# The projection of the next batch is computed beside the recurrence's chunks, and GpSimd issues the token loads

## The chip, the cores and the metric

The program runs on one core of one Trainium2 chip. A core has TensorE (PE in the rows), VectorE (DVE), ScalarE (ACT), GpSimd (POOL) and SyncE (SP), which here only issues transfers. Each takes its own instructions in order, and they wait for one another by semaphores. The metric is the device time of one execution in microseconds (us); lower is better.

## What is computed

A convolutional recurrence over an image turns `x` into `x1`, sixteen images of 64 channels and 1024 positions. Then comes a state-space layer over the 1024 positions ("tokens") of each image, and a layer of experts. The change touches the state-space layer. Cut down, with `x` the normalised tokens of a batch of 16:

```python
x_proj = x @ W_in                     # 64 -> 2*128
xs, z = jnp.split(x_proj, 2, axis=-1)
delta, Bv, Cv = xs @ W_delta, xs @ W_B, xs @ W_C
deltaA = jnp.exp(jnp.einsum('bld,dn->bldn', delta, A))
deltaB = jnp.einsum('bld,bln->bldn', delta, Bv)
def step(state, inp):                 # over the 1024 tokens
    dA_i, dB_i, x_i, C_i = inp
    state = dA_i * state + dB_i * x_i[:, None, :]
    return state, jnp.einsum('bdn,bn->bd', state, C_i)
y = (ys of the scan) * jax.nn.silu(z)
return y @ W_out
```

A state has 128 x 128 numbers in each batch.

## The kernel before

Five parts run one behind the other, parted by barriers: the convolution (`conv_phase`), the projection (`build_project`), the recurrence (`build_scan`), the gate (`build_gate`) and the experts. They pass data through tensors in HBM.

**The projection** goes over the 16 batches as a software pipeline (`pipelined`): the pieces of batches n to n-3 stand beside each other, all eight PSUM banks are in use, and two buffers of everything alternate. A batch is loaded (`px`), its mean over channels is taken and removed, squared, the variance is made by a second product, and ACT (square root) and DVE (reciprocal, product) normalise it. `xs` and `z` are made for the two halves of 512 positions, and from `xs` the rates (`delta`), the readout (`Cv`), and, with the roles of weights and data exchanged so that tokens lie on partitions, the steps (`delta` again), `own` (`xs` itself) and `Bv`; own times `Bv` is what enters. Rates, steps and entering tokens are each split into three bf16 parts (a cast, the rest, its cast, the rest of that), which are stored to `rates_dram`, `steps_dram` and `tokens_dram`; later products of parts restore near-f32 accuracy.

**The recurrence** cuts the tokens of a batch into 17 chunks: `CROWD` = 16 of 63 tokens and a last one of 16 (`CPB` = 17). A chunk has `GROUPS` = 8 units of 16 channels. For each unit `g` of chunk `c`

- PE makes in `enters` what enters the state into `enter_ps` (8 matmuls on loaded `steps` and `tokens`; two buffers, so it waits until the scan before the last one is done), and in `exponents` the exponents of the unit after it into `rate_ps` (4 matmuls); in the even units it contracts the states of the chunk before with the readout (`contract`: 4 matmuls on 32 columns each, into `y_ps`),
- ACT copies the end state of the chunk before into column 0 of `enter_ps` (`carry`) and takes two exponentials of the next unit (`decays_of`, into `decay`, a ring of four),
- DVE runs one `tensor_tensor_scan` over 128 x 1024 elements.

POOL spreads the loaded rates of a chunk over four masked copies (`s_wide`) and the readout into a sparse operand (`spread`). It does both once in a chunk, in the order widen, spread. SP issues the loads of a chunk three chunks ahead (`load`): 1 for rates, 8 for tokens (L797), 16 for steps (L801), 1 for the readout, and every second chunk 4 stores of y. Before the tokens it waits until PE has used up the buffers of the chunk two before. y is summed in two PSUM banks `y_ps[0]` and `y_ps[1]`, of two chunks each, and ACT moves each sheet out (`move_y`). The batch loop is a hardware loop (`Fori`) of 136 unrolled units.

Of the kernel before, what the change touches and what calls it, by code (L numbers as in the profile page):

```python
# [5 lines left out]
F32 = mybir.dt.float32  # L6
# [6 lines left out]
BATCH = 16  # L13
CH = 64
# [347 lines left out]
def gate_phase(nc, y_dram, z_dram, x1_dram, w_out, mean_w, identity, gate_w, gate_b, x2_dram, normed_dram, logit_dram):  # L362
    def scratch(name, shape, dt=F32):
# [8 lines left out]
    build_project(nc, identity=identity, readout_dram=readout, rates_dram=rates, steps_dram=steps, tokens_dram=tokens,  # L372
                  **held["project"])
    build_scan(nc, identity=identity, readout_dram=readout, rates_dram=rates, steps_dram=steps, tokens_dram=tokens,
               decays_dram=decays, y_dram=y, **held["scan"])
    build_gate(nc, y, z_dram, x1_dram, w_out, mean_w, identity, gate_w, gate_b, x2_dram, normed_dram, logit_dram)


def build_project(nc, x1_dram, w_in, w_delta, w_b, w_c, mean_w, readout_dram, z_dram, identity,
                  rates_dram, steps_dram, tokens_dram):  # L380

    with ExitStack() as ctx:
        def sb(name, shape, dt=F32):
            return ctx.enter_context(nc.sbuf_tensor(name, shape, dt))

        sem = Semaphores(nc, ctx, "proj")
        win = sb("win", [128, CHUNKS, 2 * INNER])
        wdelta, wc, wmean = sb("wdelta", [INNER, INNER]), sb("wc", [INNER, INNER]), sb("wmean", [128, 128])  # L390
        wtok = sb("wtok", [INNER, 3, 128])
        eps = sb("eps", [128, 1])
        x = [sb(f"px{i}", [128, BANK]) for i in range(2)]
        centred, square, std = sb("centred", [128, BANK]), sb("square", [128, BANK]), sb("std", [128, BANK])
        normed = [sb(f"normed{i}", [128, BANK]) for i in range(2)]
        xs = [sb(f"xs{i}", [INNER, CHUNKS, BANK]) for i in range(2)]
        z = [sb(f"z{i}", [INNER, CHUNKS, BANK]) for i in range(2)]
        readout = [sb(f"readout{i}", [INNER, CHUNKS, BANK]) for i in range(2)]
        parts = [sb(f"parts{i}", [INNER, SPLITS, CHUNKS, BANK], BF16) for i in range(2)]
        rest = [sb(f"rest{c}", [INNER, BANK]) for c in range(CHUNKS)]  # L400
        own = [sb(f"own{c}", [128, TILES, INNER]) for c in range(CHUNKS)]
        enters = [sb(f"enters{c}", [128, TILES, STATE]) for c in range(CHUNKS)]
        enters_left = [sb(f"enters_left{c}", [128, TILES, STATE]) for c in range(CHUNKS)]
        steps_left = [sb(f"steps_left{c}", [128, TILES, INNER]) for c in range(CHUNKS)]
        steps = [sb(f"steps{i}", [128, CHUNKS * TILES, SPLITS, INNER], BF16) for i in range(2)]
        tokens = [sb(f"tokens{i}", [128, CHUNKS * TILES, SPLITS, STATE], BF16) for i in range(2)]

        def ps(name):
            return ctx.enter_context(nc.psum_tensor(name, [128, BANK], F32))

        mean_ps, var_ps, xs_ps, zc_ps, delta_ps = (ps(n) for n in ("mean_ps", "var_ps", "xs_ps", "zc_ps", "delta_ps"))
        tok_ps = [ctx.enter_context(nc.psum_tensor(n, [128, TILES, 128], F32)) for n in ("step_ps", "own_ps", "b_ps")]

        weights_in, eps_set = sem("weights_in"), sem("eps_set")
        x_in = [sem(f"x_in{i}") for i in range(2)]
        stored = [sem(f"stored{i}") for i in range(2)]
        tok_stored = [sem(f"tok_stored{i}") for i in range(2)]
        mean_ready, centred_ready, square_ready, var_ready, std_ready = (
            sem("mean"), sem("centred"), sem("square"), sem("var"), sem("std"))
        inverse_ready, normed_ready = sem("inverse"), sem("normed")  # L420
        in_ready, xs_ready, z_ready = sem("in_ready"), sem("xs_ready"), sem("z_ready")
        out_ready, part1_ready, rest1_ready, part2_ready, part3_ready = (
            sem("out_ready"), sem("part1"), sem("rest1"), sem("part2"), sem("part3"))
        readout_ready = sem("readout")
        own_ready = sem("own")
        tok_ready, enters_ready, step1_ready, token1_ready, step_left, token_left, step2_ready, token2_ready, tok3_ready = (
            sem("tok"), sem("enters"), sem("step1"), sem("token1"), sem("step_left"), sem("token_left"), sem("step2"),
            sem("token2"), sem("tok3"))
        STORES = 2 + SPLITS
        TOK_STORES = 1 + SPLITS  # L430
        WEIGHTS = 6 + CHUNKS
        block = ctx.enter_context(nc.Block())

        def of_chunk(tile, c, a):
            return tile[:, TILES * c:TILES * c + TILES, a, :]

        @block.sync
        def _(sp):
            for s in sem.made:
                sp.sem_inc(s, START)  # L440
            for d, s in ((wdelta, w_delta), (wc, w_c), (wmean, mean_w)):
                sp.dma_start(d[:, :], s).then_inc(weights_in, DMA)
            for k, s in enumerate((w_delta, identity, w_b)):
                sp.dma_start(wtok[:, k, :], s).then_inc(weights_in, DMA)
            for c in range(CHUNKS):
                sp.dma_start(win[:, c, :], w_in[c, :, :]).then_inc(weights_in, DMA)

            def load(b, i, turn):
                sp.wait_ge(centred_ready, START + turn * 2)
                for c in range(CHUNKS):  # L450
                    sp.dma_start(x[i][CH * c:CH * c + CH, :],
                                 x1_dram[bass.ds(b, 1), :, BANK * c:BANK * c + BANK].rearrange("b c l -> (b c) l")
                                 ).then_inc(x_in[i], DMA)

            def store(b, i, turn):
                sp.wait_ge(z_ready, START + (b + 1) * CHUNKS)
                sp.dma_start(z_dram[bass.ds(b * CHUNKS, CHUNKS), :, :].rearrange("n p l -> p n l"), z[i][:, :, :]
                             ).then_inc(stored[i], DMA)
                sp.wait_ge(readout_ready, START + (b + 1) * CHUNKS)
                sp.dma_start(readout_dram[bass.ds(b, 1), :, :].rearrange("b n l -> (b n) l"),  # L460
                             readout[i][:, :, :].rearrange("p c l -> p (c l)")).then_inc(stored[i], DMA)
                sp.wait_ge(part3_ready, START + (b + 1) * CHUNKS)
                for a in range(SPLITS):
                    dst = rates_dram[bass.ds(b, 1), :, SPLITS * a:SPLITS * a + terms_of(a), :]
                    sp.dma_start(dst.rearrange("b d e l -> (b d) e l"),
                                 parts[i][:, 0:terms_of(a), :, :].rearrange("p a c l -> p a (c l)")
                                 ).then_inc(stored[i], DMA)
# [208 lines left out]
def build_scan(nc, readout_dram, a_t, identity, rates_dram, steps_dram, tokens_dram, decays_dram, y_dram):  # L676
# [4 lines left out]
    with ExitStack() as ctx:  # L681
# [85 lines left out]
        def _(sp):  # L767
            for s in sem.made:
                sp.sem_inc(s, SCAN0)
# [824 lines left out]
```

## Time and profile before

| | us |
|---|---|
| median of 3 runs | 7372.27 (7366.63 to 7378.81) |
| the profiled execution | 7362.99 |
| its span in the trace | 7361.1 |
| convolution, to the last vector instruction | 0 to 1885.6 |
| projection and the set-up of the recurrence, to the first scan | 1885.6 to 2277.1 |
| recurrence, first to last large scan | 2277.1 to 7007.2 |
| gate, experts | 7030 to 7361 |

Busy time over the span: PE 6408.9 (87%), DVE 6478.1 (88%), ACT 4524.9 (61%), POOL 2747.4 (37%). These shares are means over parts with different limits; what bounds a part is read within it. The execution is one core's, with a mean granted TensorE clock of 0.97 of full speed.

### The profile page before, as it was taken

To read this page: it belongs to the slowest core of one execution; us is meant where nothing else is said; L and a number is where in the kernel's file an instruction comes from. 1 tells how busy PE (TensorE), PEld (TensorE's weight loads), DVE (VectorE), ACT (ScalarE), POOL (GpSimd) and SP (SyncE) were. 2 spreads that over 40 slices of the span, in tenths; PEclk is the share of its full clock that TensorE was granted. 3 is DMA by queue.
4 is the path that set the end of the run, shared out by engine and by line. 5 is a ranking of instruction groups with operands and counts; after the bars stand their busy time and mean duration, and the time that the engine had idled before them with its cause. 6 is when DMAs were issued, how large, how long until landed. Compare 5 with 4: busy or idle time off the path is not lost. (4 is left out here: it accounts for less than half of the span.)

```text
span 7361.1 us, 173597 instructions
## 1 busy us (share of the span) xinstructions
PE 6408.9 (87%) x52385; PEld 3911.8 (53%) x52385; DVE 6478.1 (88%) x4166; ACT 4524.9 (61%) x9561; POOL 2747.4 (37%) x1996
## 2 busy tenths in 40 slices
PE   8999999999786888888888888888888888888867
PEld 3555547555344555555555555555555555555535
DVE  7888878888557999999999999999999999999962
ACT  7888868888464555555555555555555555555541
POOL 5555445555234333333333333333333333333300
PEclk9999999999898999999999999999999999999985
DMA  6666666666693111111111111111111111111154
GB/s 144 153 156 154 155 144 155 154 154 155 199 321 83 27 27 27 28 27 27 28 26 27 28 27 28 27 27 28 27 26 28 26 29 27 27 27 28 27 171 113
DMA packets 918664, 569.20 MB, mean 77 GB/s; under 512 B 710606, under 2 KB 819054, under 8 KB 917870
## 3 DMA queue, kind: packets, MB, share of 16 engines
q1 hardware_dynamic: 917885, 560.17, 32.1%
q8 instruction: 325, 5.32, 0.3%
q14 instruction: 454, 3.71, 0.2%
HBM read 161.99 MB, written 125.17 MB: 39 GB/s over the span
## 5 line engine op out<-in xcount | busy, mean ns | idle before, releaser
L1059 DVE TENSOR_TENSOR_SCAN states<-decay,enter_ps 128x1024 f32<-128x1024 f32 x2048 | 4468.2, 2262 | 172.3 <-ACT enter_ps L965 167.2
L876 PE MATMUL enter_ps<-s_steps,s_tokens 128*128 128x128 bf16 (+1 forms) x16384 | 2139.3, 311 | 625.6 <-DVE states L1059 514.5
L876 PEld LDWEIGHTS enter_ps<-s_steps,s_tokens 128*128 128x128 bf16 (+1 forms) x16384 | 1596.2, 130 | 1738.5 <-DVE states L1059 1569.4
L950 ACT ACTIVATE decay<-rate_ps 128x504 f32<-128x504 f32 x4096 | 2196.3, 588 | 98.0 <-PE rate_ps L854 23.8
L1016 POOL TENSOR_SCALAR s_wide<-s_rates,mask 128x512 bf16<-128x512 bf16 (+1 forms) x1088 | 1619.5, 1506 | 488.3 <-DMA s_rates<-rates_dram 353.8
L965 ACT COPY enter_ps<-states 128x16 f32<-128x16 f32 x1920 | 363.1, 189 | 1655.4 <-PE enter_ps L876 1649.6
L854 PE MATMUL rate_ps<-s_wide,s_decays 128*128 128x256 bf16 x8192 | 1330.9, 285 | 34.4 <-POOL s_wide L1016 33.7
L243 POOL TENSOR_TENSOR entered<-gates 128x512 f32<-128x512 f32 x512 | 900.9, 1760 | 888.8 <-ACT gates L203 888.8
L900 PE MATMUL y_ps<-states,spread 128*32 128x512 f32 x8320 | 1117.9, 609 | 0.4 <-issue 0.4
L1022 POOL COPY spread<-s_readout 128x64 f32<-128x64 f32 (+1 forms) x272 | 63.6, 234 | 2565.4 <-PE y_ps L900 2009.9
L854 PEld LDWEIGHTS rate_ps<-s_wide,s_decays 128*128 128x128 bf16 x8192 | 897.5, 119 | 95.8 <-issue 36.8
L161 PE MATMUL pre<-rows,weights_left 128*32 128x512 f32 x8192 | 914.0, 595 | 36.5 <-POOL rows L236 23.7
L161 PE MATMUL pre<-rows,weights_right 128*32 128x512 f32 x8192 | 910.4, 594 | 0.0
L281 DVE TENSOR_TENSOR feat<-gates,squashed 128x512 f32<-128x512 f32 x512 | 903.9, 1765 | 1.4 <-ACT squashed L210 1.4
L161 PEld LDWEIGHTS pre<-rows,weights_left 128*32 128x32 f32 x8192 | 479.1, 109 | 444.7 <-issue 373.8
L203 ACT ACTIVATE gates<-pre,biases_left 128x512 f32<-128x512 f32 x1024 | 619.5, 688 | 135.5 <-PE pre L161 135.5
L203 ACT ACTIVATE gates<-pre,biases_right 128x512 f32<-128x512 f32 x1024 | 619.8, 688 | 126.2 <-PE pre L161 126.2
L161 PEld LDWEIGHTS pre<-rows,weights_right 128*32 128x32 f32 x8192 | 485.0, 109 | 398.9 <-issue 322.8
L266 DVE TENSOR_TENSOR forgot<-gates,cell 128x512 f32<-128x512 f32 x512 | 356.6, 697 | 260.8 <-ACT gates L203 260.6
L273 DVE TENSOR_TENSOR cell<-forgot,entered 128x512 f32<-128x512 f32 x512 | 347.3, 678 | 2.3 <-POOL entered L243 2.3
L210 ACT ACTIVATE squashed<-cell 128x512 f32<-128x512 f32 x512 | 330.8, 646 | 5.6 <-DVE cell L273 5.6
L900 PEld LDWEIGHTS y_ps<-states,spread 128*32 128x32 f32 x8320 | 164.1, 108 | 211.6 <-issue 208.1
(154 smaller groups left out, 2310.4 us busy)
## 6 DMA issues: line engine op xcount, KB each, us to landing
rows<-feat SPq DMA_DIRECT2D x1024, 132.0 KB, 2.4
rows<-feat SPq DMA_DIRECT2D x512, 128.0 KB, 2.4
s_steps<-steps_dram SPq DMA_DIRECT2D x4096, 8.0 KB
rows<-feat SPq DMA_DIRECT2D x512, 127.8 KB, 2.4
s_rates<-rates_dram SPq DMA_DIRECT2D x256, 128.0 KB, 2.6
s_tokens<-tokens_dram SPq DMA_DIRECT2D x2048, 16.0 KB
rates_dram<-parts SPq DMA_DIRECT2D x32, 768.0 KB, 4.6
steps_dram<-steps SPq DMA_DIRECT2D x32, 768.0 KB, 8.0
```

Source lines behind the costliest of these rows:

```text
L161: mm = pe.matmul(pre[c][32 * q:32 * q + 32, g, :], weights[side(s)][:, 32 * g:32 * g + 32], image(rows[s][:, q, :], MARGIN + CIMG * c), st ...
L203: a = act.activation(gates[k % GATE_RING][:, g, :], pre[k % CHUNKS][:, g, :], ACT.Sigmoid, bias=biases[side(k // CHUNKS)][:, g:g + 1])
L243: pool.tensor_tensor(entered[c][:, :], gates[k % GATE_RING][:, 2, :], gates[k % GATE_RING][:, 3, :], ALU.mult).then_inc(entered_ready, 1)
L266: dve.tensor_tensor(forgot[c][:, :], gates[k % GATE_RING][:, 1, :], cell[s][:, BANK * c:BANK * c + BANK], ALU.mult).then_inc(forgot_ready, 1)
L281: dve.tensor_tensor(image(feat[s][:, :], CIMG * c), gates[k % GATE_RING][:, 0, :].rearrange("p (h w) -> p h w", w=SIDE), squashed[c][:, :] ...
L854: mm = pe.matmul(rate_ps[h][:, QUAD * q:QUAD * q + QUAD, :], decays[:, g, 2 * h + q, :], wide[s][:, g, :, :], start=True, stop=True)
L876: mm = pe.matmul(out.rearrange("p h l -> p l h"), tokens[s][0:n * TERMS, k, :], steps[s][0:n * TERMS, k, 0:n, d:d + half], start=True, sto ...
L900: mm = pe.matmul(y_ps[q % 2][32 * j:32 * j + REACH, :].rearrange("p (r d) -> p d r", r=QUAD), spread[s][:, at:at + REACH], steps_of.rearra ...
L950: act.activation(decay[i][:, HEADS // 2 * h:HEADS // 2 * (h + 1), 1:], rate_ps[h][:, :, 0:n], ACT.Exp).then_inc(decay_ready, 1)
L965: act.copy(enter_ps[i][:, :, 0], start).then_inc(carried, 1)
L1016: w = pool.tensor_scalar(wide[s][:, :, i, 0:n], rates[s][:, :, 0:n], mask[:, i:i + 1], None, ALU.mult)
L1059: dve.tensor_tensor_scan(out, factor, term, 0.0, ALU.mult, ALU.add).then_inc(scanned, 1)
```

## The change

The separate projection goes. `build_scan` takes its weights and buffers, and a batch's projection becomes a list of 16 `STAGES`, each of which fills one PSUM bank (`work_ps`, named `stage_ps` in the program) and is drained from it. The bank is the one that `y_ps[1]` had; y now has one bank, so the first contraction of a sheet waits for the move of the sheet before (`y_moved`). All 16 stages of batch 0 run ahead of the recurrence. From then on stage c of batch b+1 stands in chunk c of batch b: PE fills in unit 1 (`fill`), ACT makes the first bf16 part in unit 2, drains the bank in unit 3 into `moved`, makes the first part of what enters in unit 5 and the second part in unit 7. What DVE did (centring, the rests of the splits, the entering product) POOL now does (`differences`), from SBUF. The variance is made with tokens on partitions, so that DVE's reciprocal covers 128 x 8 elements, and PE spreads the result back by 8 small matmuls in unit 5 of chunk 1 (`fill_inverse`); the ACT square root stands in chunk 1 of every batch. SP stores each stage's result behind the loads, and waits for all of them (`projected`) ahead of the first load of the next batch. The 8 token loads of a chunk move from SP to POOL (`load_tokens`), between widen and `differences`.

```diff
+        STAGES = ((MEAN, 0), (VARIANCE, 0), (OWN, 0), (OWN, 1), (RATES, 0), (RATES, 1), (READOUT, 0), (READOUT, 1),
+                  (STEPS_OF, 0), (OWN_TOKENS, 0), (ENTERS, 0), (STEPS_OF, 1), (OWN_TOKENS, 1), (ENTERS, 1), (Z, 0), (Z, 1))
@@ PE, unit()
+                if g == 1 and c < len(STAGES) and not ending:
+                    fill(b + 1, c)
+                if g == 5 and c < len(STAGES) and not ending:
+                    fill_inverse(b + 1, c)
@@ ACT, unit()
+                if c < len(STAGES) and not ending:
+                    if g == 2:
+                        first_part(b + 1, c)
+                    elif g == (3 if STAGES[c][0] != VARIANCE else 6):
+                        drain(b + 1, c)
+                    elif g == 5:
+                        first_part_entering(b + 1, c)
+                    elif g == 7:
+                        second_part(b + 1, c)
@@ POOL
+            def differences(b, n):
...
+                elif n in SPLIT:
+                    if kind == ENTERS:
+                        pool.wait_ge(drained, stages_to(b, n + 1))
+                        pool.tensor_tensor(own[:, :], own[:, :], moved[:, :], ALU.mult).then_inc(entered, 1)
...
+                    pool.tensor_tensor(shaped(n, rest), shaped(n, own if kind == ENTERS else moved), part(n, 0), ALU.subtract
+                                       ).then_inc(left_ready, 1)
+                    pool.wait_ge(second_ready, splits_to(b, n) + 1)
+                    pool.tensor_tensor(part(n, 2), shaped(n, rest), part(n, 1), ALU.subtract).then_inc(third_ready, 1)
...
+            def batch(b, ending):
+                for c in range(CPB):
+                    if c + 1 < CPB:
+                        widen(b, c + 1)
+                        load_tokens(b, c + 1)
...
+                    if c < len(STAGES) and not ending:
+                        differences(b + 1, c)
+                    if c + 1 < CPB:
+                        spread_out(b, c + 1)
@@ SP, batch()
+                    if c < len(STAGES) and not ending:
+                        store_stage(b + 1, c)
+                    if c == 4 and not (isinstance(b, int) and b + 2 >= BATCH):
+                        load_x(b + 2)
                     if c == CROWD - 3 and not ending:
+                        projected(b + 1)
                         load(b + 1, 0)
```

On PE, unit 1 of a chunk (`x4` and the like count equal rows; `stage_ps` is the work bank). Before, units 0 and 1:

```order
L876 MATMUL enter_ps<-s_steps,s_tokens 128x16x8 x6
L876 MATMUL enter_ps<-s_steps,s_tokens 128x15x8 x2
L854 MATMUL rate_ps<-s_wide,s_decays 128x256 x4
L900 MATMUL y_ps<-states,spread 32x128x4 x4
L876 MATMUL enter_ps<-s_steps,s_tokens 128x16x8 x6
L876 MATMUL enter_ps<-s_steps,s_tokens 128x15x8 x2
L854 MATMUL rate_ps<-s_wide,s_decays 128x256 x4
```

and now, in a chunk whose stage is a Z:

```order
L763 MATMUL enter_ps<-s_steps,s_tokens 128x16x8 x6
L763 MATMUL enter_ps<-s_steps,s_tokens 128x15x8 x2
L740 MATMUL rate_ps<-s_wide,s_decays 128x256 x4
L787 MATMUL y_ps<-states,spread 32x128x4 x4
L763 MATMUL enter_ps<-s_steps,s_tokens 128x16x8 x6
L763 MATMUL enter_ps<-s_steps,s_tokens 128x15x8 x2
L740 MATMUL rate_ps<-s_wide,s_decays 128x256 x4
L705 MATMUL stage_ps<-normed,win 128x512
```

One 128 x 512 f32 matmul stands behind the odd unit, which had no contraction.

On POOL, one chunk of the recurrence with the semaphores that are waited for. Before:

```order
L1013 REGISTER_ALU [waits scan_rates_in1]
L1016 TENSOR_SCALAR s_wide<-s_rates,mask 128x8x64 [waits scan_rate_ready]
L1016 TENSOR_SCALAR s_wide<-s_rates,mask 128x8x64 x3
L1019 REGISTER_ALU [waits scan_readout_in1]
L1022 COPY spread<-s_readout 128x16x4 [waits scan_y_summed]
```

and now, in chunk 10, whose stage is ENTERS:

```order
L983 REGISTER_ALU [waits scan_rates_in1]
L986 TENSOR_SCALAR s_wide<-s_rates,mask 128x8x64 [waits scan_rate_ready]
L986 TENSOR_SCALAR s_wide<-s_rates,mask 128x8x64 x3
...
L1000 DMA s_tokens<-tokens_dram 16x4x128 x3
L1000 ISA
L1000 DMA s_tokens<-tokens_dram 16x4x128 x2
L968 REGISTER_ALU
L969 TENSOR_TENSOR own<-own,moved 128x512 [waits scan_drained]
L973 REGISTER_ALU [waits scan_third]
L974 TENSOR_TENSOR rest<-own,parts 128x512 [waits scan_first]
L977 TENSOR_TENSOR parts<-rest,parts 128x4x128 [waits scan_second]
```

Eight token loads and up to three products or differences stand between widen and spread; spread follows behind.

On SP, the loads of one chunk. Before:

```order
L790 ISA [waits scan_widened1]
L790 DMA s_rates<-rates_dram 128x8x64
L792 ISA
L797 ISA [waits scan_enter_ready]
L797 DMA s_tokens<-tokens_dram 16x4x128 x3
```

and now:

```order
L624 ISA [waits scan_widened0]
L624 DMA s_rates<-rates_dram 128x8x64
L626 REGISTER_ALU
L631 ISA [waits scan_enter_ready]
L631 DMA s_steps<-steps_dram 8x4x128
```

The 16 step loads follow at once on the wait that stood ahead of the tokens.

## Rows read from the trace of the kernel before

**Rows 1.** Stretches: us, busy us and count by engine, granted clock, DMA share, GB/s.
```profile
1960.00:2220.00 260.00, 205.95 (x906) 125.14 (x905) 156.60 (x172) 158.30 (x282) 85.75 (x67) 0.94 0.94 322
...
3166.00:3461.00 295.00, 250.31 (x2068) 161.32 (x2067) 282.09 (x135) 168.49 (x405) 104.64 (x86) 0.99 0.14 27
```

**Rows 2.** Groups: line, engine, operation, out<-in, count; busy us, mean ns; idle before.
```profile
L1059 DVE TENSOR_TENSOR_SCAN states<-decay,enter_ps 128x1024 f32<-128x1024 f32 x2048 | 4468.2, 2262 | 172.3 <-ACT enter_ps L965 167.2 <-ACT decay L950 4.8
```

**Rows 3.** Timeline, a pair of units: start, us, engine, line, operation, idle before.
```profile
2999.54 13.15 DVE L1059 TENSOR_TENSOR_SCAN states<-decay,enter_ps 128x1024 f32<-128x1024 f32 x6
...
3003.26 1.07 PE L900 MATMUL y_ps<-states,spread 128*32 128x512 f32 x8
...
3004.26 1.03 PE L876 MATMUL enter_ps<-s_steps,s_tokens 128*128 128x128 bf16 x8
...
3005.33 0.19 ACT L965 COPY enter_ps<-states 128x16 f32<-128x16 f32 x1 [1.11 <-PE enter_ps L876]
...
3006.21 1.03 PE L876 MATMUL enter_ps<-s_steps,s_tokens 128*128 128x128 bf16 x8 [0.48 <-DVE states L1059]
```

**Rows 4.** Timeline of DVE behind the start of a batch.
```profile
4352.89 52.39 DVE L1059 TENSOR_TENSOR_SCAN states<-decay,enter_ps 128x1024 f32<-128x1024 f32 x24 [3.75 <-ACT enter_ps L965]
...
4412.12 226.60 DVE L1059 TENSOR_TENSOR_SCAN states<-decay,enter_ps 128x1024 f32<-128x1024 f32 x104 [6.84 <-ACT enter_ps L965]
```

**Rows 5.** Timeline of SP, the loads of chunk 3 of that batch.
```profile
4395.02 0.41 SPq L790 DMA_DIRECT2D s_rates<-rates_dram  x1
4395.82 5.48 SPq L797 DMA_DIRECT2D s_tokens<-tokens_dram  x8
4401.48 7.28 SPq L801 DMA_DIRECT2D s_steps<-steps_dram  x16
```

**Rows 6.** Who waited for whom, whole trace: us, times, longest.
```profile
PE enter_ps L876 <- DMA s_steps<-steps_dram: 84.9, 39, 4.4
```

**Rows 7.** Timeline around the projection: end of the convolution, first scan.
```profile
1884.86 0.76 DVE L303 SCALAR_TENSOR_TENSOR x<-pre,skip_b,rows 64x512 f32<-64x512 f32 x1 [0.96 <-PE pre L178]
...
2277.07 2.29 DVE L1059 TENSOR_TENSOR_SCAN states<-decay,enter_ps 128x1024 f32<-128x1024 f32 x1 [19.43 <-ACT enter_ps L965]
```

**Rows 8.** Lines asked by themselves: count, ns min/median/max; matmul records are two per product.
```profile
L515 PE MATMUL delta_ps<-xs,wdelta x64: 592/592/668, 1920.1 to 2211.3; 128*128 128x512 f32 x64
...
L597 POOL TENSOR_TENSOR square<-centred x16: 1038/1482/1484, 1900.6 to 2180.6; 128x512 f32<-128x512 f32 x16
...
L622 DVE TENSOR_TENSOR normed<-centred,std x16: 691/692/694, 1909.2 to 2187.8; 128x512 f32<-128x512 f32 x16
...
L797 SPq DMA_DIRECT2D s_tokens<-tokens_dram x2176: 495/557/1732, 2262.8 to 6987.7; - x198
...
L1059 DVE TENSOR_TENSOR_SCAN states<-decay,enter_ps x2048: 2259/2260/2289, 2277.1 to 7007.2; 128x1024 f32<-128x1024 f32 x187
```

**Rows 9.** Groups of the projection on PE and ACT, and a table load of the gate.
```profile
L527 PE MATMUL step_ps<-wtok,xs 128*128 128x128 f32 x256 | 51.1, 282 | 5.1 <-DVE steps_left L645 5.1
...
L515 PE MATMUL delta_ps<-xs,wdelta 128*128 128x512 f32 x64 | 33.9, 611 | 16.7 <-DVE rest L628 16.7
...
L558 ACT CAST parts<-delta_ps 128x512 bf16<-128x512 f32 x32 | 18.6, 582 | 24.8 <-PE delta_ps L515 24.8
...
L1208 ACT ACT_TABLE_LOAD x15 | 19.2, 1283 | 35.7 <-PE g_var_ps L1182 35.6
```

**Rows 10.** Timeline of POOL in mid-batch.
```profile
3008.88 0.24 POOL L1022 COPY spread<-s_readout 128x64 f32<-128x64 f32 x1 [10.83 <-PE y_ps L900]
...
3026.30 0.24 POOL L1022 COPY spread<-s_readout 128x64 f32<-128x64 f32 x1 [10.40 <-PE y_ps L900]
3026.63 6.18 POOL L1016 TENSOR_SCALAR s_wide<-s_rates,mask 128x512 bf16<-128x512 bf16 x4
```

**Rows 11.** The page, DMA issues: KB each, median us to landing.
```profile
rates_dram<-parts SPq DMA_DIRECT2D x32, 768.0 KB, 4.6
...
s_readout<-readouts_dram SPq DMA_DIRECT2D x256, 32.0 KB, 1.8
```

## What the change will do to the time: the prediction on record

> **What bounds the kernel now.** I read the stretches first. Inside the recurrence DVE is busy 282 of 295 us, PE 250, ACT 168, POOL 105 [rows 1]; inside the projection no engine is full, DMA is at 0.94 of its engines, and the stretch costs what it costs beside nothing else. The group of scans says the same: 2048 scans with 172 us of idle time before them, 167 of it put down to ACT's carry [rows 2]. A scan that lasts 2.26 us follows the last one every 13.15/6 = 2.19 us [rows 3], so a chunk of eight takes 17.5 us. The recurrence is bound by DVE, the projection by its own chain, and the two add up: from the end of the convolution, 1885.6, to the first scan, 2277.1, are 391 us in which no scan runs [rows 7]. Then I asked the timeline what little DVE waits for. Behind the start of a batch it stands still 6.84 us ahead of chunk 3 [rows 4]. SP begins that chunk's tokens at 4395.82 and its steps only 5.7 us later, ending at 4408.8 [rows 5]; PE's wait for steps is 84.9 us in all [rows 6].
>
> **The start.** The 16 batches' projection outside the recurrence becomes one. I sum the 16 stages of batch 0 one behind the other, since one bank serves all. A fill is 33.9/32 = 1.06 us for 512 columns [rows 9], 1.3 with the hand-over and a clock that starts low; a copy by ACT 0.6 [rows 9]; a POOL difference 1.04 undisturbed [rows 8]. Eight plain stages (own, readout, own tokens, z, each twice) at 2.0 make 16. Six split stages at 1.3 + 0.6 + 0.6 + 1.04 + 0.6 = 4.2, entering tokens with 1.7 more twice, make 28. Mean 4.0 (two POOL operations), variance 7.5 with a table load of 1.28 [rows 9]: 56 us. The set-up of the recurrence stands beside this, save some 15 us until the weights and zeroed buffers are there. Stores that a ring of two waits for, and the last one, add 10 (a rates store lands in 4.6 [rows 11], three are issued one by one). From there loads 2.5, widen 6.2 [rows 10], eight token loads 8 and their landing 2, first matmuls and carry 2: 21. First scan at 1885.6 + 15 + 56 + 10 + 21 = 1988, less some 8 for fills beside the last part of a split: 1980. That is 297 us earlier (267 to 312 by the bounds of these pieces).
>
> **SP loses eight issues per chunk.** Its 16 step loads of chunk 3 begin 5.7 us earlier [rows 5], and the steps are no longer late. In 15 of 16 batches that gives 5.7 us: minus 85, which is also the whole wait of PE [rows 6]. The stage stores it gets instead, three transfers at most, stand behind the loads and in chunks where it has time. `projected` holds SP in chunk 13 until stage 13 has landed, about 5 us, while the loads behind it are wanted two chunks later: nothing. What covers it is those two chunks.
>
> **PE and ACT.** Behind an even unit, with its contraction from 3003.26, the next enters begin at 3004.26, 0.3 us later than the scan that frees their buffer; behind an odd unit they begin at 3006.21 after 0.48 us of idle time [rows 3]. So a pair of units has 0.5 us free, a chunk 2.0. The carry that an enters at +0.3 feeds ends 1.26 later, at 1.6 of 2.19: 0.5 us in hand. A fill of 1.06 behind unit 1 puts the next enters at about +0.8, and the one after at +1.0, which is 0.15 us too late; then two odd units have paid it back. Token stages are four small products, at most 4 x 51.1/128 = 1.6 us [rows 9], but these durations overlap; I take the same. 14 stages x 0.15 x 15 batches: plus 30 us (bounds 0, and 120 at 1.3 us for each fill). ACT has 0.8 us free in a unit and gets one or two copies of 0.6 in a few. The stage of the variance has more: a square root among exponentials loads a table twice, 1.28 each [rows 9], and unit 5 gets eight small products; about 1.3 us a batch, plus 20.
>
> **POOL.** Here the sum is decided. Spread for a chunk comes free with the contraction, 1.6 us ahead of the chunk's end, and widen follows it by 0.3 and takes 6.18 [rows 10]: it ends 4.9 us into the next chunk. Then come eight token issues of t each, behind which are queued the differences (ACT waits for those, and behind ACT the carry), spread, and the next widen. The trace has no transfer issued by POOL. Its nearest row is SP's token issue, 0.56 us median (0.68 with the gaps, 5.48/8), 1.73 at most [rows 5, 8]. Those are my ends. POOL takes 1.50 times as long as DVE for the same product (1038 against 692 ns [rows 8]), and 1.5 x 0.68 = 1.0 is what I take. Three kinds of chunk:
> In a plain one the tokens have landed at 4.9 + 8t + 2. PE wants them at unit 7, 15.4, and has 0.5 in hand: late by 8t - 9.0.
> After a split stage POOL first makes the last part, 1.15 us behind ACT's cast in unit 7, so widen starts some 1.6 us later: late by 8t - 7.4, six times a batch.
> In the two ENTERS stages the product must be ready for ACT in unit 5, at 11.6; it is ready at 4.9 + 8t + 1.04, and ACT's copy of 0.6 then stands ahead of a carry that had 0.3 to spare: late by 8t - 6.4.
> At t = 1.0 this is 6 x 0.6 + 2 x 1.6 = 6.8 us a batch, x15 = plus 102. At 0.8 it is nothing, at 1.1 it is 200, at 1.2 (6 x 2.2 + 2 x 3.2 + 9 x 0.6 = 25) some 375, at 1.3 about 590.
> The Trainium skill, DMA: Bandwidth & Descriptors, "Latency and other measured facts", gives GpSimd's software-made descriptors about 1 us to the first byte and SP's 0.6: no run here shows the first; scaled to 0.68 it would be an estimate of 1.13 us an issue and a total near 7270.
>
> **Sum.** Span 7361.1 - 297 - 85 + 30 + 20 + 102 = 7131. The execution has 1.9 us around its span, and the median of the runs stands 9.3 us over the profiled one: 7142.
>
> **Rivals.** *POOL hides it all* (t under 0.9): without the 102, 7040. For it: POOL is idle 190 of 295 us [rows 1]. Against: its idle time lies between widen and spread, where all the new work goes in one piece.
> *PE and ACT pay in full*: fills of 1.3 us, 0.5 us per chunk, 120 for the 30: 7232. For it: only 0.48 us free in every second unit [rows 3].
> *POOL becomes the bound*, the slower side: with an issue of 1.17 us or more the loop spread, widen, eight issues, landing, enters is longer than DVE's chunk, and each chunk is stretched. Break-even: what the other terms give, 332 us over 15 batches, is 22 us a batch, which t = 1.17 costs. At 1.3 it is 7630, at 1.73 every chunk is 4.8 us longer and more, beyond 8000. For it: the longest issues even on SP reach 1.73 [rows 8], and GpSimd is the slow engine here. Against: that row is one of SP's extremes.
> *POOL is locked out by DVE.* Beside DVE's projection work the same POOL product took 1482 ns for 1038 [rows 8]. If the scans did this to POOL's two-input operations or to its issues, the ENTERS chunks would lose 0.5 to 1 us, and with every issue waiting out a scan a chunk would take 26 us: over 9000. Against: scans last 2259 to 2289 ns [rows 8] with widen beside them, and widen 1.55 each. The skill, SBUF — State Buffer, "SBUF: two separate sides", has a lock between the two engines only for a DVE operation in a two-port mode or with two SBUF inputs; a scan reads one from SBUF and one from PSUM, and by that rule nothing is lost.
> *The stages do not hide*, because the single bank passes through PE, ACT and POOL in order: it has a chunk of 17.5 us for a chain of 4 to 8, so only a late POOL brings this, and it is in the third rival.
>
> **How the numbers follow.** Forecast with t from 0.9 to 1.13, 7060 to 7260: 0.42. POOL hides all: 0.14. PE and ACT in full: 0.12. POOL the bound: 0.28, the last part of it beyond 7540. Locked out: 0.04. Faster by over 0.2% (about 15 us, what a measurement here can tell): the first three and a shade of the fourth, 0.69; within 0.2%: 0.04, where the fourth crosses break-even; slower 0.27. The range runs from 6990 (t under 0.9, the start at 1965, free fills) to 7540 (t = 1.25); some 0.06 is left below and 0.14 above.
>
> **What would show it.** The first scan at about 1980. Token issues on POOL with a mean of 1.0. DVE's scans still 2.19 us apart in most units, with short gaps in unit 6 of chunks 10 and 13 (carry waits) and at the start of chunks behind a split stage. No gap ahead of chunk 3 from steps. If the issues cost over 1.17, PE's longest wait will be the tokens, in every chunk, and the forecast is wrong on the side of slower; if PE's enters begin more than 1 us behind the scans in units 2 and 3, the fills were priced too low.

## The result and the profile after

| | before | after |
|---|---|---|
| median of 4 runs each | 7375.54 (7366.63 to 7379.01) | 6976.08 (6968.81 to 6985.00) |
| span of the profiled execution | 7361.1 | 6983.2 |
| first large scan starts | 2277.1 | 1976.5 |
| last large scan starts | 7007.2 | 6624.7 |

The ratio is 0.9461, 95% interval 0.9444 to 0.9477: 5.4% faster, where 3.1% was forecast, and 14 us below the low end of the range. The span lost 377.9 us: 300.6 ahead of the first scan, 81.9 within the recurrence (4730.1 to 4648.2), and 4.6 came back in the parts behind it.

The page's first part, and two of its queues:

```profile
PE 6360.4 (91%) x52737; PEld 4064.9 (58%) x52737; DVE 6283.9 (90%) x3973; ACT 4598.9 (66%) x9719; POOL 4052.5 (58%) x4364
...
q1 hardware_dynamic: 780925, 525.96, 31.9%
q0 software_dynamic: 69632, 34.22, 2.3%
```

POOL has 1305 us more work, 1104 of them its token issues, whose transfers are q0. PE has hardly less than before, since nearly the same products are made. What is new is the place: fifteen of the sixteen batches' projections now lie beside scans. The mid-recurrence stretch of [rows 1] (us, then busy of PE, PEld, DVE, ACT, POOL) shows it:

```profile
1905.00:1960.00 55.00, 32.49 (x88) 18.08 (x88) 0.20 (x1) 15.81 (x29) 19.28 (x17) 0.50 0.37 121
...
3166.00:3461.00 295.00, 269.24 (x2199) 175.45 (x2198) 286.50 (x140) 188.73 (x445) 193.15 (x238) 0.99 0.21 49
```

DVE went from 282.1 to 286.5 of 295 us although PE, ACT and POOL all carry more. The upper row is the one projection left ahead of the recurrence: its granted clock is 0.50, the lower of the two levels (1.2 GHz), where the sixteen batches before had 0.94 [rows 1].

The group of the scans, which answers to [rows 2]:

```profile
L1070 DVE TENSOR_TENSOR_SCAN states<-decay,enter_ps 128x1024 f32<-128x1024 f32 x2048 | 4466.1, 2268 | 134.1 <-ACT enter_ps L901 129.9 <-ACT decay L886 2.6
```

The token issues, now on POOL, asked by themselves as in [rows 8] (ns min/median/max), and their landing:

```profile
L1000 POOL DMA_DIRECT2D s_tokens<-tokens_dram x2176: 481/508/723, 1967.9 to 6615.1; - x198
...
DMA to landing us min/median/max: 1.7/2.1/4.3
```

The timeline of DVE (start and duration in us, idle time before it in brackets): the first scan, then a batch's start, then what follows it.

```profile
1976.46 2.29 DVE L1070 TENSOR_TENSOR_SCAN states<-decay,enter_ps 128x1024 f32<-128x1024 f32 x1 [67.13 <-ACT enter_ps L901]
...
3432.27 4.47 DVE L1070 TENSOR_TENSOR_SCAN states<-decay,enter_ps 128x1024 f32<-128x1024 f32 x2 [3.81 <-ACT enter_ps L901]
3438.02 21.97 DVE L1070 TENSOR_TENSOR_SCAN states<-decay,enter_ps 128x1024 f32<-128x1024 f32 x10 [1.28 <-ACT enter_ps L901]
3460.18 220.08 DVE L1070 TENSOR_TENSOR_SCAN states<-decay,enter_ps 128x1024 f32<-128x1024 f32 x101
...
5796.67 252.75 DVE L1070 TENSOR_TENSOR_SCAN states<-decay,enter_ps 128x1024 f32<-128x1024 f32 x116
```

116 scans in 252.75 us are 2.18 each, as before [rows 3]: through fourteen stages and the entering chunks DVE does not wait once. The waits left stand at a batch's start and in its short last chunk (37.7 us in all there, 34.5 before). The one ahead of the first scan (67.1 us, 19.4 before [rows 7]) belongs to the start; without it the scans' idle time fell from 152.9 to 67.0 us. The wait for steps of [rows 6] is gone. SP's largest wait shows its new freedom (before it was 147.3 us, 82 times, longest 5.3):

```profile
SPq L627 <- PE enter_ps L763: 1400.2, 226, 18.5
```

### The profile page after: what moved, and what is told of

The parts are those of the page before. It is cut to its first block and busy times, and to the rows that moved or that the text cites. A ratio compares the mean times of both kernels' runs of the same rounds, so it can differ in the third digit from the quotient of the medians.

```text
span 6983.2 us, 175886 instructions
## 1 busy us (share of the span) xinstructions
PE 6360.4 (91%) x52737; PEld 4064.9 (58%) x52737; DVE 6283.9 (90%) x3973; ACT 4598.9 (66%) x9719; POOL 4052.5 (58%) x4364
## 3 DMA queue, kind: packets, MB, share of 16 engines
q0 software_dynamic: 69632, 34.22, 2.3%
## 5 line engine op out<-in xcount | busy, mean ns | idle before, releaser
L1000 POOL DMA_DIRECT2D s_tokens<-tokens_dram x2176 | 1103.9, 514 | 26.4 <-issue 22.7
L161 PEld LDWEIGHTS pre<-rows,weights_left 128*32 128x32 f32 x8192 | 547.1, 109 | 376.8 <-issue 215.7
L161 PEld LDWEIGHTS pre<-rows,weights_right 128*32 128x32 f32 x8192 | 557.2, 109 | 326.5 <-issue 165.3
L1009 POOL COPY spread<-s_readout 128x64 f32<-128x64 f32 (+1 forms) x272 | 64.4, 237 | 751.9 <-PE y_ps L787 650.4
L977 POOL TENSOR_TENSOR parts<-rest,parts 128x512 bf16<-128x512 f32 x96 | 111.0, 1156 | 423.6 <-ACT parts L871 423.6
```

Of the source, the lines that this page charges most:

```text
L161: mm = pe.matmul(pre[c][32 * q:32 * q + 32, g, :], weights[side(s)][:, 32 * g:32 * g + 32], image(rows[s][:, q, :], MARGIN + CIMG * c), st ...
L1000: pool.dma_start(tokens[s][e::TERMS, :, :], src).then_inc(tokens_in[s], DMA)
```

## The experiments

Each ratio is to the kernel before, run on the same chip beside the experiment. "The changed kernel" is the one with the whole change.

**Who pays for the token loads.** The two theories: the eight issues are what GpSimd is short of time for, or they are SP's burden and GpSimd has room. First the changed kernel with them back on SP, and the kernel before with only them moved:

```diff
@@ e1_tokens_on_sp, SP load() of the changed kernel; POOL's load_tokens calls go
+                for e in range(TERMS):
...
+                    sp.dma_start(tokens[s][e::TERMS, :, :], src).then_inc(enter_in[s], DMA)
@@ e2_before_tokens_pool, kernel before: the same lines leave SP, and in POOL behind widen
+                pool.wait_ge(enter_ready, units_to(b, before(c) + 1))
...
+                    pool.dma_start(tokens[s][e::TERMS, :, :], src).then_inc(tokens_in[s], DMA)
```

> The changed kernel with the 8 token loads of a chunk put back on SyncE, ahead of the 16 step loads as before the change; nothing else is touched. Theory A: moving them to GpSimd is what took DVE's waits inside the recurrence from 205 us (19 of them ahead of the first scan) to 102 us beside the first one; the waits ahead of chunk 3 come back, and since SyncE now also stores the stages, more chunks are late: 7060 to 7120 us against 6976. Theory B: the waits went for another reason (the order of the loop's code, one y bank, earlier rates): 6976 within 15 us.

> The kernel before with one thing of the change alone: GpSimd issues the 8 token loads of a chunk, behind widen. Theory A: the waits for steps ahead of chunk 3 of a batch go, 80 us less: 7285 to 7310. Theory B: nothing, 7375 within 15 us. An issue on GpSimd should take 0.51 us here too.

Measured: 7199.38 us (0.9775 [0.9759, 0.9791]) and 7268.45 us (0.9872 [0.9855, 0.9888]), the first slower and the second faster than either theory had it. The move alone gives the kernel before some 95 us, close to the forecast's 85. Inside the changed kernel its absence costs 223 by the medians (232 by the ratios), over twice that. The scans of e2, as a group and asked by their line:

```profile
L1064 DVE TENSOR_TENSOR_SCAN states<-decay,enter_ps 128x1024 f32<-128x1024 f32 x2048 | 4462.4, 2261 | 77.1 <-ACT enter_ps L963 72.2 <-ACT decay L948 4.9
...
L1064 DVE TENSOR_TENSOR_SCAN states<-decay,enter_ps x2048: 2259/2260/2289, 2282.4 to 6912.3; 128x1024 f32<-128x1024 f32 x187
```

The recurrence of e2 is 4629.9 us long, 100.2 shorter than before and 18.3 shorter than the changed kernel's 4648.2. So inside the recurrence the move gave 100, and the rest of the change, the stages beside the scans above all, took 18 back. Some 10 of these are waits at the batches' starts (65 us over 15 starts in the changed kernel, 55 in e2), and 4 are DVE's reciprocals; what makes the longer waits was not tested.

SP's timeline of e1, the last chunk of a batch, and a rates load fifteen chunks later:

```profile
3217.72 0.41 SPq L624 DMA_DIRECT2D s_rates<-rates_dram  x1
3218.47 5.68 SPq L631 DMA_DIRECT2D s_tokens<-tokens_dram  x8
3224.34 7.28 SPq L635 DMA_DIRECT2D s_steps<-steps_dram  x16
3231.91 0.36 SPq L640 DMA_DIRECT2D s_readout<-readouts_dram  x1
3232.94 2.67 SPq L647 DMA_DIRECT2D y_rows_dram<-y_sb  x4
3238.59 0.43 SPq L624 DMA_DIRECT2D s_rates<-rates_dram  x1
...
3487.17 0.39 SPq L624 DMA_DIRECT2D s_rates<-rates_dram  x1
```

and, among the waits of e1 (us, times, longest):

```profile
PE enter_ps L766 <- DMA s_steps<-steps_dram: 192.8, 88, 5.5
...
SPq L627 <- PE enter_ps L766: 95.5, 36, 5.7
```

From one rates load to the next are 20.9 us here, 3.0 of them a gap behind the last store, for which no wait is shown; this is the place where SP's loop jumps back. From 3217.72 to 3487.17 are fifteen chunks of 17.96 us each. DVE's recurrence in e1 (1972.6 to 6845.5) has the same pace, 17.99 a chunk, against 17.16 in the changed kernel, and SP hardly waits for PE's buffers any more (95.5 us, against 1400.2). With the stores of the stages added to the tokens, SP's queue is the bound in most chunks. So the stages come in at their low price only because the tokens went.

**GpSimd's time ahead of the tokens.** The measured issue is 0.51 us and not 1.0. To see whether the formula for lateness was right and only t wrong, clears of an unused buffer stretch the same place:

```diff
@@ POOL, load_tokens(), ahead of the eight issues (e4: two of 128 x 2336; e5, e6: three of 2180 and 2570)
+                for j in range(2):
+                    pool.wait_ge(idled, SCAN0 + (b * CPB + c) * 2 + j)
+                    pool.sem_inc(passed, 1)
+                    pool.memset(idle[:, :], 0.0).then_inc(idled, 1)
```

> The changed kernel with 4.0 us of GpSimd work (two memsets of an unused tile) ahead of the 8 token issues of each chunk, so that widen, issues and what is behind them stand as if an issue took 1.0 us, the value that the prediction took, and not the measured 0.51. Theory A, the prediction's step on GpSimd with its own formula: late by 8t - 7.4 after a split stage and 8t - 6.4 in an ENTERS chunk: plus 106 us, 7080. Theory B: the formula was too strict as well, GpSimd has that much room: within 15 us of 6976.

> The changed kernel with some 5.8 us of clears by GpSimd ahead of the token loads (three, a little smaller than in the run with 7.0): issues of 4.07 and clears make about 10.0 us, an issue of 1.25 us each. Theory A, the prediction's formula (15 times the sum of what exceeds 7.4 six times, 6.4 twice, 9.0 nine times a batch): at 10.0, +477: 7453. Theory B, the two neighbours joined: +135 at 8.25 and +590 at 11.03, the formula's +752 there being cut because a late chunk leaves GpSimd no wait for the contraction ahead of spread: at 10.0 about +420: 7396 (7370 to 7425). Both lie above the kernel before, 7365, so that the point from which GpSimd takes back all that the change gives lies under 1.25 us an issue; the formula said 1.17.

> The changed kernel with three clears of an unused buffer by GpSimd, some 6.6 us in all by the 2.0 us each that two smaller ones took, between widen and the token loads of each chunk of the batches. Everything else is as in the changed kernel. Eight issues at 0.51 us are 4.1 us, so this puts the tokens where issues of 1.33 us would have put them. Theory A, the prediction's formula for GpSimd's lateness holds beyond its small values: at 1.33 the six chunks behind a split stage lose 3.2 us each, the two entering ones 4.2 and nine plain ones 1.6, 42 us a batch, 15 batches, +630: 7600 (7540 to 7700), slower than before by 3%, which is the rival 'POOL the bound'. Theory B, a chunk that is late leaves the next one later too, since the loop spread, widen, issues, spread is then longer than the chunk: more than the formula, 7750 or beyond. Theory C, stalls of DVE give GpSimd time back, so that one late chunk covers the next: under 7450.

Issues and clears together took 8.25, 10.07 and 11.03 us (for "8t"; 4.07 without clears). The loss is worked out as the difference of the ratios times 7375:

| 8t | t | formula, 15 batches | measured | time, ratio to before |
|---|---|---|---|---|
| 4.07 | 0.51 | 0 | 0 | 6976.08, 0.9461 |
| 8.25 | 1.03 | 132 | 144 | 7110.89, 0.9656 [0.964, 0.9672] |
| 10.07 | 1.26 | 495 | 402 | 7378.32, 1.0006 [0.9996, 1.0015] |
| 11.03 | 1.38 | 740 | 591 | 7566.01, 1.0262 [1.0244, 1.028] |

At 8.25 the total is near the formula's; no run tells where between 4.07 and 8 the loss begins. Farther out the formula says nearly a quarter too much. The break-even with the kernel before is at t = 1.26 and not 1.17; some 0.04 of these 0.09 are there because the other terms gave 399 us and not 332, at which the formula itself would have said 1.21. Why the far end is cheaper was not settled. One thing that the formula leaves out is seen: POOL's waits for the contraction ahead of spread fall from 650.4 us to 214.2, 104.5 and 83.6 as the clears grow. In their place the waits of e4 bear the formula out only in part. DVE's timeline has one ahead of unit 6 of an entering chunk (chunk 13 here) and a shorter one ahead of the chunk behind it; further down is the next batch's start:

```profile
3123.37 4.46 DVE L1075 TENSOR_TENSOR_SCAN states<-decay,enter_ps 128x1024 f32<-128x1024 f32 x2 [2.15 <-ACT enter_ps L902]
3128.30 34.95 DVE L1075 TENSOR_TENSOR_SCAN states<-decay,enter_ps 128x1024 f32<-128x1024 f32 x16 [0.47 <-ACT enter_ps L902]
...
3174.80 2.29 DVE L1075 TENSOR_TENSOR_SCAN states<-decay,enter_ps 128x1024 f32<-128x1024 f32 x1 [4.54 <-ACT enter_ps L902]
3179.65 2.29 DVE L1075 TENSOR_TENSOR_SCAN states<-decay,enter_ps 128x1024 f32<-128x1024 f32 x1 [2.56 <-ACT enter_ps L902]
3183.28 21.97 DVE L1075 TENSOR_TENSOR_SCAN states<-decay,enter_ps 128x1024 f32<-128x1024 f32 x10 [1.35 <-ACT enter_ps L902]
```

Summed over the whole timeline, the waits ahead of unit 6 in the two entering chunks are 63 us, where the formula has 56. Ahead of the other chunks but the first they are 16, where it has 76 for the ones behind a split stage. And the batches' starts have 45 us more than in the changed kernel, which the formula does not have at all. That the total came out within 12 us is in part luck.

Two of e4's waits, for the entering product and for the tokens:

```profile
ACT parts L867 <- POOL own L970: 101.5, 32, 3.4
PE enter_ps L764 <- DMA s_tokens<-tokens_dram: 73.0, 81, 3.2
```

**What an issue costs.** Is 0.51 us the price of an instruction, or of what is moved by it (64 pieces of 256 bytes)?

```diff
@@ e9_split_issues, POOL load_tokens()
-                    pool.dma_start(tokens[s][e::TERMS, :, :], src).then_inc(tokens_in[s], DMA)
+                    h = max(blocks[s] // 2, 1)
+                    for k in range(0, blocks[s], h):
+                        pool.dma_start(tokens[s][e::TERMS, k:k + h, :], src[:, k:k + h, :]).then_inc(tokens_in[s], DMA)
```

> The changed kernel with each token load of the 63-token chunks made as two DMAs of half the blocks on GpSimd (16 issues of half the size for 8; the same bytes and descriptors in all). Theory A, the 0.51 us of an issue are per instruction: 16 issues take 8.2 us, 4.1 us more per chunk, as the clears of 4.0 us did: 7090 to 7130. Theory B, they are per descriptor (64 of 256 bytes each): 16 issues of 0.26 us, 6976 +-20. In between the time tells the fixed part.

Measured: 7056.56 us (0.9575 [0.9558, 0.9591]), 84 more than the changed kernel. POOL's timeline has sixteen issues in 7.98 us:

```profile
3343.75 7.98 POOL L1002 DMA_DIRECT2D s_tokens<-tokens_dram  x16
```

and the line asked by itself has the same median of 508 ns at half the size:

```profile
L1002 POOL DMA_DIRECT2D s_tokens<-tokens_dram x4224: 481/508/727, 1967.4 to 6692.3; - x192
```

So at these sizes the price does not follow the bytes or the pieces, and both theories' times, 7090 to 7130 and 6976, were missed. What stays the same with the instruction is the queue's packets, 32 an issue in both kernels (69632 for 2176 above, and here 135168 for 4224), so that a price per packet is not excluded:

```profile
q0 software_dynamic: 135168, 34.35, 2.9%
```

This is also a fifth point for the formula: 8t = 7.97 gives 98.

**How much room PE has for a fill.** The forecast charged 0.15 us per chunk; the trace shows nothing. Here each stage's matmuls stand two or three times:

```diff
@@ PE, fill(b, n, times), called with times = 2 (e7) or 3 (e8) in unit 1
-                    mm = pe.matmul(work_ps[:, :], win[:, c, at:at + INNER], normed[:, :], start=True, stop=True)
+                    for _ in range(times):
+                        mm = pe.matmul(work_ps[:, :], win[:, c, at:at + INNER], normed[:, :], start=True, stop=True)
```

> The changed kernel with each matmul of a stage issued twice in the batches' chunks (same operands, same result), so a stage's fill in unit 1 costs PE twice its time: 1.06 us more for 512 columns. Theory A, PE's free time: the trace shows 2.0 us of PE idle per chunk, 0.5 behind each odd unit, and the two buffers ahead of DVE let a fill be paid back over the next units; a fill of 2.1 us puts the enters of units 2 and 3 some 1.6 to 2.1 us late against DVE's need and the carry has 0.5 in hand: 0.3 to 1.1 us lost in each of 14 chunks of 15 batches, +60 to +230: 7040 to 7200. Theory B, the slack is per chunk and not per unit, and only 2.0 us in all counts: nothing, 6976 +-15. The prediction's price rule (lost = what exceeds the 0.5 in hand after 0.3, so 0.15 at 1.06) would give 1.2 us at 2.1: +250, 7230.

> The changed kernel with each matmul of a stage issued three times in the batches' chunks: 2.1 us more of PE per chunk. With two times the run took 123 us more than the changed kernel, 0.59 us in each of 14 chunks of 15 batches, for 1.06 us more. Theory A, a threshold in the place (what exceeds 1.06 + 0.47 = 1.53 us of fill is paid one for one): 0.59 + 1.06 = 1.65 us a chunk, +346: 7322 (7280 to 7360). Theory B, PE's free time per chunk is what counts (2.0 us, and with 2.1 it is used up): then twice already stood at the edge, and three times costs 1.2 us a chunk: +250, 7225. Theory C, every microsecond added costs 0.55 of it from the first on (then the single fill cost some 0.5 us a chunk too, and the free fill of my theory is wrong): +245, 7220, and a kernel without a fill would be 120 us faster than the changed one.

Measured: 7098.85 us (0.9632 [0.9615, 0.9648]) and 7282.6 us (0.9871 [0.9856, 0.9886]). Against the changed kernel that is 126 and 302 us by the ratios, or 0.60 and 1.44 in each of 14 x 15 chunks. In DVE's timeline of e7 every chunk of eight scans has the same wait in the same place:

```profile
3394.03 17.75 DVE L1072 TENSOR_TENSOR_SCAN states<-decay,enter_ps 128x1024 f32<-128x1024 f32 x8 [0.30 <-ACT enter_ps L903]
3412.08 17.75 DVE L1072 TENSOR_TENSOR_SCAN states<-decay,enter_ps 128x1024 f32<-128x1024 f32 x8 [0.30 <-ACT enter_ps L903]
```

and in e8's:

```profile
3284.23 17.75 DVE L1072 TENSOR_TENSOR_SCAN states<-decay,enter_ps 128x1024 f32<-128x1024 f32 x8 [1.09 <-ACT enter_ps L903]
3303.07 17.75 DVE L1072 TENSOR_TENSOR_SCAN states<-decay,enter_ps 128x1024 f32<-128x1024 f32 x8 [1.09 <-ACT enter_ps L903]
```

A chunk takes 18.05 us in e7 and 18.84 in e8, and 220.08 x 8/101 = 17.43 in the changed kernel's row from 3460.18: the second fill costs 0.6 us, the third 0.8 (0.84 by the times, 176/210). If each fill takes 0.8, a place with T of room loses 2 x 0.8 - T = 0.6, so T = 1.0, and one fill stays 0.2 below it. (These are estimates from two differences.) It is a threshold, as theory A of e8 has it, with smaller numbers. Theory C, the same share from the first fill on, doesn't fit a third fill that costs more than the second, and B and C both gave some 250 where 302 were measured. No run of the changed kernel leaves the single fill out. The changed kernel's timeline gives nearly the same price without subtraction, at a stage of four small products:

```profile
3022.26 13.16 DVE L1070 TENSOR_TENSOR_SCAN states<-decay,enter_ps 128x1024 f32<-128x1024 f32 x6
...
3026.11 1.06 PE L710 MATMUL stage_ps<-wtok,xs 128*128 128x128 f32 x8
...
3027.01 1.02 PE L763 MATMUL enter_ps<-s_steps,s_tokens 128*128 128x128 bf16 x8
...
3031.12 1.03 PE L763 MATMUL enter_ps<-s_steps,s_tokens 128*128 128x128 bf16 x8 [0.26 <-DVE states L1070]
```

The row says 1.06 us, but the next enters begin 0.90 after the fill did. They stand 0.37 us behind the scan that began at 3026.64 (3022.26 + 2 x 2.19), not 0.8, and two units later PE waits for DVE again.

**One bank for y.** The kernel before with y in one bank:

```diff
-                    pe.wait_ge(y_moved, SCAN0 + b * SHEETS + max(q - 1, 0))
+                    pe.wait_ge(y_moved, SCAN0 + b * SHEETS + q)
```

> The kernel before with y in one PSUM bank and the wait for the move of the sheet before, as the change has it; nothing else. The prediction priced this at nothing, since ScalarE moves a sheet in unit 7 and its next carry stands behind the move: 7375 within 15 us. If PE waited for the move in each of the 9 sheets of a batch for 0.3 us or more, 7420 or more.

Measured: 7367.39 us (1.0003 [0.9993, 1.0012]). The second bank was free to give away.

**The waits that are left.** In the changed kernel a batch that starts behind a jump of the hardware loops waits longer than the one unrolled boundary (1.7 us). Two or seven batches in one turn take jumps away:

```diff
@@ e10_two_per_loop, all five engines (PE shown); e11_seven_per_loop has 7 for 2
-            with pe.Fori(1, BATCH - 1) as b:
-                for u in range(UPB):
-                    unit(b, u, False, False)
+            with pe.Fori(0, (BATCH - 2) // 2) as turn:
+                for j in range(2):
+                    for u in range(UPB):
+                        unit(turn * 2 + 1 + j, u, False, False)
```

> The changed kernel with two batches in one turn of the hardware loops of all five engines, so that 7 of 14 jumps back go (in the trace each costs DVE 2.5 to 3.3 us at a batch's start more than the 1.7 us of the one boundary that is unrolled). Theory A, jumps cost what the boundaries show: 7 x 2.5 to 3.3 = minus 17 to 23, 6953 to 6959. Theory B, what is lost at a batch's start is the chain of loads, not the jump: 6976 +-5. Theory C, a longer body makes each jump or its code loading dearer: slower than 6985.

> The changed kernel with seven batches in one turn of the hardware loops, so 2 turns in place of 14: 12 jumps back fewer. Two per turn gave 24 us for 7 jumps, 3.4 each. Theory A, jumps cost the same each: minus 41, 6935 (6930 to 6940). Theory B, a body of seven batches outgrows something that two do not (instructions read from memory in a new place): as with two per turn, 6952, or slower.

Measured: 6952.3 us (0.9432 [0.9419, 0.9446]) and 6936.51 us (0.9404 [0.9391, 0.9417]). That is 24 us for 7 jumps and 40 for 12 (21 and 42 by the ratios), 3.0 to 3.5 each, and e11 is the fastest kernel of this study. In the changed kernel's timeline PE and ACT both stand still behind the jump with nothing that released them:

```profile
3432.71 1.03 PE L763 MATMUL enter_ps<-s_steps,s_tokens 128*128 128x128 bf16 x8 [2.46 <-issue]
...
3432.06 0.17 ACT L901 COPY enter_ps<-none 128x16 f32<-128x16 f32 x1 [2.45 <-issue]
```

In e11, DVE's timeline at a boundary without a jump has 1.60 us ahead of the batch's first scan, and nothing behind it where the changed kernel had 3.81 and 1.28:

```profile
3418.67 26.32 DVE L1075 TENSOR_TENSOR_SCAN states<-decay,enter_ps 128x1024 f32<-128x1024 f32 x12 [1.60 <-ACT enter_ps L903]
```

## Why the prediction was wrong, step by step

By its own sum, in the span:

| term | forecast | measured | |
|---|---|---|---|
| start | -297 | -300.6 | right |
| SP's eight issues | -85 | -100 | by e2 (4730.1 to 4629.9) |
| PE's fills | +30 | 0 | mis-sized: no wait in the stages' chunks |
| variance stage | +20 | +4 | mis-sized |
| POOL | +102 | 0 | t was half of what was taken |
| batches' starts and the rest, against e2 | 0 | +14 | not in the sum |
| behind the recurrence | 0 | +4.6 | |

The differences add up to 148 us, which is 7131 against 6983; the median then stood 9 us below the profiled execution and not 9 above it, and that makes the 166 us to 6976.

**The start** was right as a sum with errors inside that cancel. Up to where the first stage's drain begins it took 17.6 us (15 forecast), from there to the end of the last drain 54.7 (56 + 10 - 8 = 58), and then loads, widen, issues and landing 18.6 (21). The clock was lower than thought: at 0.50 a fill takes 2.05 us where 1.3 was forecast (592 ns a record at the least and 1192 at the most for the same product). The eight issues took 4.25 us and not 8.

**SP's issues** went as forecast in place, and nearly in size: 100 by e2 for 85. The scans' idle time without the first wait fell by 85.9 in the changed kernel, which looks like an exact hit but is the move less what the rest of the change took back. What the forecast did not have is that they were also what made room for the stage stores: without the move the changed kernel would have been at 7199 (e1).

**PE.** The step that failed is "a fill of 1.06 behind unit 1 puts the next enters at about +0.8". The 1.06 is the sum of modelled durations of overlapping records; as a delay of the next instruction it is 0.8 to 0.9 (e7, e8, and 3027.01 - 3026.11). The Trainium skill (Perfetto Trace Analysis, the note at its head) calls matmul busy time a bad measure, since matmuls are pipelined; the runs agree, with 0.8 of cost for 1.06 of busy time. At that price the enters come at +0.37, hardly later than the +0.3 of before, from which the same paragraph had 0.5 in hand. The mechanism, a threshold behind which what exceeds it is paid, fits e7 and e8.

**The variance stage** was priced by its table loads on ACT. The scans beside it run without a wait; what it costs is DVE's own reciprocal, a 0.18 us instruction that sets the next scan back by 0.27: 15 x 0.27 = 4.

**POOL** was the decisive step, and what failed in it is "1.5 x 0.68 = 1.0 is what I take": measured are 0.51 us an issue, and with them none of the 102 us. The ratio of 1.5 came from an elementwise product, and says nothing of how fast an engine hands over a transfer. SP's own median of 0.56, the row nearest in kind, was named as one end and was nearer the truth, though the truth is still below it. The figure of the Trainium skill (DMA: Bandwidth & Descriptors, "Latency and other measured facts"), about 1 us for GpSimd's descriptors against 0.6, is a time to the first byte; read as a price per issue it gave 1.13, and the trace has 0.51. The landing, 2.1 us in the median, was as assumed. The rule for the lateness at t near 1.0 was right in its total (e4: 144 us where it gives 132) and only in part in its places: the entering chunks were right, the chunks behind a split stage hardly lost anything, and the batches' starts were missing.

**The rivals.** "POOL hides it all" is what happened, with 7040 as its price because it kept the 30 and the 20. "POOL the bound" is real too, but its break-even is at t = 1.26 (e5). "DVE locks POOL out" does not show: POOL's square of 1038 ns [rows 8] takes 1.04 us beside scans too, and the new product 1.27 us ahead of the recurrence and 1.28 within it, by POOL's timeline after:

```profile
1940.20 1.27 POOL L969 TENSOR_TENSOR own<-own,moved 128x512 f32<-128x512 f32 x1 [2.59 <-ACT moved L859]
...
1986.33 1.04 POOL L962 TENSOR_TENSOR square<-centred 128x512 f32<-128x512 f32 x1
...
3324.20 1.28 POOL L969 TENSOR_TENSOR own<-own,moved 128x512 f32<-128x512 f32 x1
```
The rule of the Trainium skill (SBUF — State Buffer, "SBUF: two separate sides"), by which a scan with one input in PSUM locks nothing, agrees with that.

**The range** failed on its low side by 14 us. Its low end took the earliest start and free fills, but kept the whole 20 for the variance stage and the 9 between profile and median as if they were known. Each cost that no row of before shows should have reached zero there. A lower t would not have moved it, since by the formula POOL costs nothing from 0.8 down.

## What to carry to other kernels

Work that had a stretch of its own goes beside a bound engine for little (18 of 4648 us here) as long as every queue that it passes through keeps its place in the period; ask for each queue whether its sum over a period stays below the bound engine's, and then how late it makes the one thing that is waited for. GpSimd's issue of a transfer cost 0.51 us whether it moved 16 or 8 KB, so issues can go from a full queue to it, and should not be split. A total that agrees is not yet a rule confirmed: look whether the waits lie where the rule puts them. Where a step hangs on a cost that no row shows, take the row nearest in kind, not a ratio from another kind of work.

## What was not expected of the hardware

GpSimd issued a transfer in 0.51 us, beside running scans as well, faster than SP (0.68 with gaps), and it landed in 2.1 us. Each jump of the hardware loops of the five engines cost 3.0 to 3.5 us of the recurrence. TensorE was granted 0.50 of full speed through the one projection that is left ahead of the recurrence, and 0.94 through most of the sixteen of before.
